# A two-layer transformer block on one core: order of the score maxima, weight splits and output projection, the first keys in two halves, and the rotation's halves exchanged by transfers

## The reference

```python
xn = _layernorm(x)
x = x + attn0(xn) + ffn0(xn)      # softmax(q k / 4) v, then Wo; gelu(xn W1 + b1) W2 + b2
xn = _layernorm(x)
x = x + attn1(xn) + ffn1(xn)      # below; silu(x1) * x2, then w3

def _rope(x, cos, sin):           # on q and k of layer 1
    x1, x2 = jnp.split(x, 2, axis=-1)
    rot = jnp.concatenate([-x2, x1], axis=-1)
    return x * cos + rot * sin
```

## Time and profile before

| | us |
|---|---|
| median of 3 runs | 607.77 |
| lowest, highest | 606.92, 608.82 |
| profiled execution, whole | 603.88 |
| its span | 602.2 |
| PE busy in the span | 566.0 |
| DVE busy | 456.7 |
| ACT busy | 348.2 |
| POOL busy | 234.2 |

### The profile page before, as it was taken

The page is one execution under the profiler, slowest core; times in us unless marked ns, Lnnn a source line. Parts: engine busy times, 40 slices in busy tenths (PEclk is TensorE's granted clock), DMA queues, the critical chain, the costliest instruction groups (busy, mean ns, idle before and its releaser), DMA issues.

```text
span 602.2 us, 10503 instructions
## 1 busy us (share of the span) xinstructions
PE 566.0 (94%) x3216; PEld 435.4 (72%) x3216; DVE 456.7 (76%) x1232; ACT 348.2 (58%) x598; POOL 234.2 (39%) x345
## 2 busy tenths in 40 slices
PE   4899899999999999999999998989989999998997
PEld 3797567877777878668777676867667778775764
DVE  6499876856466687476898687798989889789673
ACT  3666746673564673675674666447645664556451
POOL 6143414623203421213223114354745486455242
PEclk9989999999999999999999999999999999999999
DMA  6987442244223244315434314335443354444101
GB/s 199 128 247 226 119 116 81 80 140 109 89 67 107 82 129 124 89 41 170 124 123 123 89 47 130 89 90 129 136 108 87 99 161 130 106 124 113 29 3 70
DMA packets 30535, 67.02 MB, mean 111 GB/s; under 512 B 4880, under 2 KB 18192, under 8 KB 28560
## 3 DMA queue, kind: packets, MB, share of 16 engines
q1 hardware_dynamic: 21840, 38.04, 24.3%
q0 software_dynamic: 8640, 28.32, 15.7%
HBM read 50.87 MB, written 13.63 MB: 107 GB/s over the span
## 4 chain that ended last, share of the span: by engine, by line
PE 69%; DVE 12%; issue 6%; DMA 5%; ACT 5%; POOL 2%; SPq 0%; DVEq 0%; ACTq 0%; POOLq 0%
PE banks L763 47%; PE banks L823 7%; PE banks L849 6%; PE banks L871 6%; DMA q_sb<-max_t 3%; DVE banks L1153 2%; DMA q_sb<-stage 1%; DVE x_res L1197 1%; ACT L1004 1%; DVE hid L1218 1%; PE banks L783 1%; PE banks L852 1%; POOL probs L705 1%; DVE bn L1051 1%; ACT hid_f L1005 1%
## 5 line engine op out<-in xcount | busy, mean ns | idle before, releaser
L985 ACT ACTIVATE probs<-banks 128x512 f32<-128x512 f32 (+1 forms) x256 | 138.0, 545 | 184.9 <-PE banks L849 150.1
L763 PE MATMUL banks<-xnT,w_up 128*128 128x512 f32 x576 | 151.6, 397 | 0.1
L1158 DVE TENSOR_REDUCE neg_max<-banks 128x2 f32<-128x512 f32 x128 | 87.5, 688 | 78.0 <-PE banks L823 76.2
L763 PE MATMUL banks<-w_down,hid 128*128 128x512 f32 x480 | 127.9, 400 | 5.7 <-ACT hid_f L1005 2.0
L763 PEld LDWEIGHTS banks<-xnT,w_up 128*128 128x128 f32 x576 | 101.6, 189 | 27.5 <-issue 10.3
L763 PEld LDWEIGHTS banks<-w_down,hid 128*128 128x128 f32 x480 | 85.3, 189 | 33.4 <-DVE neg_max L1158 8.9
L1153 DVE CUSTOM_DVE_ANT_0 banks<-banks,mask_qk 128x128 f32<-128x128 f32 (+1 forms) x256 | 86.4, 375 | 29.9 <-PE banks L823 29.4
L823 PEld LDWEIGHTS banks<-k_sb,q_sb 96*128 96x128 f32 x512 | 93.1, 193 | 22.0 <-issue 3.4
L823 PE MATMUL banks<-k_sb,q_sb 96*128 96x256 f32 (+1 forms) x512 | 100.4, 278 | 4.2 <-DMA q_sb<-stage 2.0
L705 POOL TENSOR_SCALAR_AFFINE_SELECT probs<-probs 128x256 f32<-128x256 f32 x128 | 61.8, 483 | 78.2 <-ACT probs L985 71.7
L849 PE MATMUL banks<-q_sb,k_sb 97*128 97x512 f32 x192 | 79.2, 412 | 9.9 <-DMA q_sb<-max_t 6.4
(11 more groups left out here) (79 smaller groups left out, 657.1 us busy)
## 6 DMA issues: line engine op xcount, KB each, us to landing
q_sb<-q_parts SPq DMA_DIRECT2D x60, 256.0 KB, 4.4
raw<-in_up POOLq DMA_DIRECT2D x48, 256.0 KB, 3.1
raw<-in_down POOLq DMA_DIRECT2D x40, 256.0 KB, 3.0
q_parts<-stage SPq DMA_DIRECT2D x30, 256.0 KB, 2.5
raw<-in_attn POOLq DMA_DIRECT2D x20, 256.0 KB, 3.6
k_parts<-stage SPq DMA_DIRECT2D x14, 256.0 KB, 2.5
k_sb<-k_parts SPq DMA_DIRECT2D x14, 256.0 KB, 4.0
out<-x_res SPq DMA_DIRECT2D x8, 256.0 KB, 2.2
```

Source lines behind the costliest of these rows:

```text
L763: mm = nc.tensor.matmul(out_ap, lhs(a), rhs(b_), start=first and j == 0, stop=stop and j == 2, **kw)
L985: nc.scalar.activation(probs[:, i, 0:w], banks[:, ST_BANKS[k % 2], 0:w], ACT.Exp, scale=SCALES[n // B]).then_inc(exp_done, 1)
L1158: nc.vector.tensor_reduce(neg_max[:, s, 2 * g:2 * g + 2, t], banks[:, bank_of[x], :].rearrange("p (r t) -> p r t", r=2)[:, :, 0:w], AX.X, ...
```

## The change

Six edits. (1) `mt` and `mrow` are appended earlier and count to the head of slot 5, so they stand ahead of the due steps. (2) The `w_out` splits of layer 0, four in slot 7 of unit 0 before, go one each to slot 7 of units 0 to 3. (3) In layer 0 the eight parts of `up` stand ahead of `wo`. (4) The first keys go in two halves of four transfers of 64 source partitions: groups 0 to 3 ahead of the first queries, groups 4 to 7 between the two halves of these; layer 0's key weights and the two places that store and load its keys are permuted to suit. (5) `turn` comes four slots after `qkv` and not two, `round` and `store` five and not four. (6) ACT starts two transfers behind its drain that put each half of `qkv_v` into the other half of `rot_b`; the two sine products of DVE go, and `turn` first multiplies `rot_b` by the sines in one instruction of 128 partitions, then adds. The signs in the sine table move with it. ACT's drain then also waits for POOL's last rounding (`staged_lo`), which DVE did before.

```diff
     if x[0] == "qkv":
-        return [(1, ("drain", x)), (2, ("turn", x)), (4, ("round", x)), (4, ("store",) + x[1:])]
+        return [(1, ("drain", x)), (4, ("turn", x)), (5, ("round", x)), (5, ("store",) + x[1:])]
...
-        head = [k for k, x in enumerate(slot) if x[0] in ("st", "m")]
+        head = [k for k, x in enumerate(slot) if x[0] in ("st", "m", "mt", "mrow")]
...
+        if i == MT_SLOT and u + 1 < UNITS:
+            slots[i] += [("mt", u + 1), ("mrow", u + 1)]
...
-    if u + 1 < UNITS:
-        slots[5] += [("mt", u + 1), ("mrow", u + 1)]
...
-        fill = parts(("wo", n - 1, 0)) + parts(("wo", n - 1, 1)) + fill
+        k = 8 if u < LU else 0
+        fill = fill[:k] + parts(("wo", n - 1, 0)) + parts(("wo", n - 1, 1)) + fill[k:]
...
-    if u == 0:
-        slots[7] += split(0, "attn", 6, 7, 8, 9)
+    if u < S:
+        slots[7] += split(0, "attn", 6 + u)
...
             if k == 2:
-                eng.wait_ge(first_k, 64)
+                for f in range(2):
+                    eng.wait_ge(first_k[f], 64)
...
+            def first_keys(f):
+                k = stg[("store", 0, 2)]
+                for h in range(2):
+                    for e in range(2):
+                        at = 32 * h + 16 * e
+                        sp_.dma_start(k_sb[at:at + HD, 4 * f:4 * f + 4, :].bitcast(F32),
+                                      stage[64 * f:64 * f + 64, k % 2, h, 0, :].bitcast(F32)).then_inc(first_k[f], 16)
...
+                            if j == 0:
+                                first_keys(1)
...
                         if n:
                             pe.wait_ge(k_loaded[f], 16 * n)
                         else:
-                            pe.wait_ge(first_k, 64)
+                            pe.wait_ge(first_k[f], 64)
...
                     ins.then_inc(wk_copied, 1)
+                    if n >= B:
+
+                        act.wait_ge(wk_copied, cp[x] + 1)
+                        if hips[x]:
+                            act.wait_ge(staged_lo, hips[x])
+                        nc.scalar.dma_start(rot_b[0:64, 0:w, :], qkv_v[64:P, 0:w, :]).then_inc(swapped, 16)
+                        nc.scalar.dma_start(rot_b[64:P, 0:w, :], qkv_v[0:64, 0:w, :]).then_inc(swapped, 16)
...
-                    dve.wait_ge(rot_sin, 2 * hips[x] + 2)
+                    dve.wait_ge(c_loaded, 48)
+                    dve.wait_ge(swapped, 32 * (hips[x] + 1))
+                    nc.vector.tensor_tensor(rot_b[:, 0:w, :], rot_b[:, 0:w, :],
+                                            table[:, 1:2, :].to_broadcast([P, w, T]), ALU.mult).then_inc(rot_sin, 1)
+                    dve.wait_ge(rot_sin, hips[x] + 1)
```

More of the change, by code:

```diff
@@ L37 @@
 RAW = 4
+MT_SLOT = 5
 RING = 3
@@ L111, in with_followers @@
 def with_followers(slots):
-    due = [[] for _ in range(len(slots) + 5)]
+    due = [[] for _ in range(len(slots) + 7)]
     o = []
     for g, slot in enumerate(slots):
-        head = [k for k, x in enumerate(slot) if x[0] in ("st", "m")]
+        head = [k for k, x in enumerate(slot) if x[0] in ("st", "m", "mt", "mrow")]
         cut = head[-1] + 1 if head else 0
@@ L447, in build @@
         m_loaded = [sem(f"m_loaded{k}") for k in range(RING)]
-        first_k = sem("first_k")
+        first_k = [sem(f"first_k{f}") for f in range(2)]
         first_q = [sem(f"first_q{j}") for j in range(2)]
+        swapped = sem("swapped")
         st_filled = sem("st_filled")
@@ L584, in _ @@
                     if x == ("store", 0, 2):
-                        for h in range(2):
-                            for e in range(2):
-                                at = 32 * h + 16 * e
-                                sp_.dma_start(k_sb[at:at + HD, :, :].bitcast(F32),
-                                              stage[:, k % 2, h, 0, :].bitcast(F32)).then_inc(first_k, 16)
+                        first_keys(0)
                     elif x == ("store", 0, 0):
@@ L602, in _ @@
                         for j in range(2):
-                            dst = kscr[n].rearrange("(h e) d (g t) -> e (d g) h t", e=2, g=NKV)[j]
+                            if n < B:
+                                dst = kscr[n].rearrange("q d x -> q (d x)").rearrange("(h e) (p t) -> e p h t", e=2, t=T)[j]
+                            else:
+                                dst = kscr[n].rearrange("(h e) d (g t) -> e (d g) h t", e=2, g=NKV)[j]
                             sp_.dma_start(dst, stage[:, k % 2, :, 0, :].bitcast(F32)).then_inc(staged[k % 2], 16)
@@ L621, in _ @@
                     g = slice(4 * f * T, (4 * f + 4) * T)
+                    if n < B:
+                        src = kscr[n].rearrange("q d x -> q (d x)").rearrange("q (f d x) -> f q d x", f=2, d=HD)[f]
+                    else:
+                        src = kscr[n].rearrange("q d x -> (q d) x")[:, g]
                     sp_.dma_start(k_sb[0:4 * HD, 4 * f:4 * f + 4, :].rearrange("p g t -> p (g t)").bitcast(F32),
-                                  kscr[n].rearrange("q d x -> (q d) x")[:, g]).then_inc(k_loaded[f], 16)
+                                  src).then_inc(k_loaded[f], 16)
                 if x[0] == "mrow":
@@ L1108, in _ @@
                                             stage[:, k % 2, 0, 0:w, :].bitcast(F32), ALU.subtract).then_inc(wk_emptied, 1)
-                if x[0] == "drain" and x[1][0] == "qkv" and x[1][1] >= B:
-                    x = x[1]
-                    _, n, pair = x
-                    w = 2 if pair < 2 else 1
-                    dve.wait_ge(wk_copied, cp[x] + 1)
-                    dve.wait_ge(c_loaded, 48)
-                    if hips[x]:
-                        dve.wait_ge(staged_lo, hips[x])
-                    other = table[:, 1:2, :]
-                    nc.vector.tensor_tensor(rot_b[0:64, 0:w, :], qkv_v[64:P, 0:w, :],
-                                            other[64:P].to_broadcast([64, w, T]), ALU.mult).then_inc(rot_sin, 1)
-                    nc.vector.tensor_tensor(rot_b[64:P, 0:w, :], qkv_v[0:64, 0:w, :],
-                                            other[0:64].to_broadcast([64, w, T]), ALU.mult).then_inc(rot_sin, 1)
                 if x[0] == "turn":
@@ L1239, in _layouts @@
     block = (REP + 2) * HD
-    w0 = np.concatenate([i["L0_attn_Wq"][q_rows(lambda h: h * HD)], i["L0_attn_Wk"][kd(lambda g: g * HD)],
+    k0 = np.array([(4 * f + g) * HD + d for f in range(2) for d in range(HD) for g in range(4)])
+    w0 = np.concatenate([i["L0_attn_Wq"][q_rows(lambda h: h * HD)], i["L0_attn_Wk"][k0],
                          i["L0_attn_Wv"][gd(lambda g: g * HD)]])
@@ L1258, in _layouts @@
     row = np.arange(P) // 8
-    rope = np.stack([cos[row % 8], np.where((row < 8)[:, None], sin[row % 8], -sin[row % 8])], 1).astype(np.float32)
+    rope = np.stack([cos[row % 8], np.where((row < 8)[:, None], -sin[row % 8], sin[row % 8])], 1).astype(np.float32)
     c = np.ascontiguousarray
```

## The result

The changed kernel takes **625.68 us** (median of 4 runs, 624.6 to 628.1) where the kernel before takes 608.3 beside it: a ratio of **1.031**, 95% interval 1.027 to 1.036, so 3% slower. The ratio is taken over fast runs alone, so it differs a little from the quotient of the two medians, 1.029. The forecast of 602.2 and its range of 595.0 to 608.8 are both missed, on the wrong side. The profiled execution took 628.07, its span 626.3 us against 602.2.

The account below looks back on a forecast made before the run. PE was taken as the bound, busy 566.0 of 602.2 us, so only its 36.2 us of idle time could be won. Terms +3.3 - 3.3 - 1.6 - 0.5 - 3.5 = -5.6 moved the median 607.77 to 602.2; range 595.0 to 608.8.

Parts of the forecast that it names:

- First keys in halves, +3.3: Start: queries land 2.9 us earlier, but ScalarE's third drain waits for keys and delays the first `m`; loss of 3.3 us.
- Splits of `w_out`, `up` ahead of `wo`, -3.3 and -1.6: Unit 1's waits of PE go, -3.3 us; layer 0's waits for a GELU, 2.0 us together, mostly go, -1.6.
- -0.5 for the maxima: Maxima ahead of due steps, outside the rotation's stretch: part of PE's 6.4 us of waits goes, -0.5 us.
- The rotation, -3.5: Units at 380 to 546: -4.7 us together with the maxima, against 0.7 for ScalarE's issues and 0.5 for `mrow`; net -3.5.
- 9.7 had been expected: Of the 12.9 us of work leaving VectorE over twelve rotations, 9.7 fall in the stretch from 380 to 546.
- half of the 9.35: PE idles 9.35 us in 380 to 546; half goes by the rotation and the maxima together, -4.7 us.
- VectorE was all of it: Rival, units at 380 to 546: all 9.35 us of PE's idle time go, instead of 3.5 net; 596.3 us, chance 0.11.
- The 0.5 for `mrow` behind the store: Rotation units: `mrow` stands behind the rotation's later store on SyncE; cost taken as 0.5 us.
- the store holds the maxima: Rival, rotation units: late store delays `mrow`, six times 1.08, 6.5 us, if rounding ends after maxima's copy; 608.7, chance 0.17.
- The exchange is late: Rival, rotation units: VectorE's turn waits for the transfers, 1.1 us nine times, 10 us; 612.2 us, chance 0.13.
- The rule on the shared port: VectorE's new product costs 618 ns by the rows, 951 if taking turns with GpSimd, giving back about 1.0 us: 603.2.

Follow-up runs that it names:

- e1: Changed kernel with each of layer 0's six half-key loads made four transfers of 16 partitions: 613.56 us, ratio 1.0097 to the kernel before.
- e3: Changed kernel with the first keys in halves undone, including order, store and load of layer 0's keys: 610.25 us, ratio 1.0049 to the kernel before.
- e12: Kernel before with only the first three edits (maxima, `w_out` splits, `up` ahead of `wo`), a repeat of e7: 596.87 us, ratio 0.9833.
- e2: Changed kernel with the rotation's store six slots after its projection instead of five: 620.41 us, ratio 1.0208 to the kernel before.
- e4: e3 with the rotation's store one slot later: 603.96 us, ratio 0.9950 to the kernel before.
- e9: e5 without the exchange transfers, the product reading `qkv_v` itself: 620.72 us, ratio 1.0228 to the kernel before.
- e5: Kernel before with only the rotation's two edits (later slots; exchange by transfers and one product): 622.76 us, ratio 1.0255.
- e6: Kernel before with only the rotation's later slots, its two products left in place and no exchange: 613.16 us, ratio 1.0097.
- e10: e3 with the rotation's rounding and store both one slot later: 610.34 us, ratio 1.0058 to the kernel before.
- e7: Kernel before with only the first three edits (maxima, `w_out` splits, `up` ahead of `wo`): 597.32 us, ratio 0.9838.

## Why the prediction was wrong, step by step

- **First keys in halves, +3.3.** The start was right in mechanism, and each of its times came within 1.0 us. Its size is less sure. The 2.9 of e1 against e3 is near the term, but the traces put only 0.9 of it at the start; the +4.1 of the first section compares two single executions, and the same start varies by nearly as much (last section). The step that failed is the other half of that edit. The prediction says nothing of the new order in which layer 0's keys are stored and loaded, and so costs it at nothing; the diff shows it, six loads with a source of four rows. It cost 13.0, nearly as much as the rotation.
- **Splits of `w_out`, `up` ahead of `wo`, -3.3 and -1.6.** Right in sign and too small. Unit 1 gained 5.1, that is all three waits and what lay in smaller ones; units 5, 9 and 13 gained 3.3 together, more than the 2.0 of the waits for the GELU. With -0.5 for the maxima the sum was -5.4, and -9.8 and -10.1 were measured.
- **The rotation, -3.5.** Wrong in sign: +13.1 beside the other three edits (e3 against e12), +15.5 alone. Its premise held in part: VectorE lost 14.0 us of work, 6.5 of them in layer 1, where 9.7 had been expected. But the step "half of the 9.35" failed. It took a wait's place for granted: a busy share of 88% was read as the cause of the waits, and the work that went stood in a unit's first slots, while the product that came stands in the slot ahead of the row maxima. In unit 16 the copy of the maxima comes 0.5 us later by that place, and TensorE's wait grows as much. How that place makes all of the 8.0 is not shown: in unit 23 the landing grew and not the copy's delay, and most of the time is the clock behind the waits. With VectorE's work gone and TensorE's idle time in layer 1 up from 15.7 to 24.6, the rival "VectorE was all of it" is out as well. The 0.5 for `mrow` behind the store measured 6.0 to 6.3 (e2, e4).
- **The rival "the store holds the maxima"** had mechanism and point of decision right: in unit 23 the store starts at 508.13, behind the copy of the maxima at 507.83. Its sum of 6.5 is close to the 6.0 and 6.3 measured, but by luck: it counted six waits of 1.08, and the store lengthened three of 2.6 to 2.7. Behind one of these, in unit 17, the clock fell to 0.50 in the changed kernel, which the prediction left out. "The exchange is late" did not come true with four slots (2.8 us of waits) and did with two (29.3). ScalarE's two issues took 0.47 and 0.92 us at the median, not 0.425 each; by e9 against e5 that made no difference that can be told.
- **The rule on the shared port** (the Trainium skill, SBUF — State Buffer, section "SBUF: two separate sides"): the new product averages 742 ns, between the 618 of the rows and the 951 of the rule. Single ones take 1.27 in the changed kernel and 1.78 in e9, the latter beside a GpSimd addition of two operands that began 0.05 us earlier; the product ends 0.55 after it. The trace agrees with the rule.

The sum as measured: +13.0 loads, +2.9 the rest of the first keys' edit, +13.1 rotation, -10.1 the other three: +18.9, the ratio of 1.031. The parts are differences along one row of kernels, so they must add up to it. By the intervals they stand to some 3 us each, and they come from different chips.

## What to carry to other kernels

When a layout is "permuted to suit", read every transfer that touches it as a new instruction with a new form, and look at who stands behind it in its queue. Taking work off an engine helps only where that engine is waited for: compare the place of the work that goes with the place of the work that comes, against the one result the bottleneck needs next. A wait of two or three microseconds on the main engine can cost twice its length when the clock falls behind it, so price it by rows that show what came after; the same length of wait can also cost nothing more.

## What the runs showed of the hardware

- One transfer of 256 KB from four long rows delays the loads behind it by microseconds: a query load took up to 11.5 us from issue to landing in the changed kernel, 6.5 in e1 and 7.5 before.
- In layer 1 one wait of 1.70 (e6) was followed by a clock of 1.00 and one of 2.70 (e9) by 0.50, 1.2 GHz, over the five microseconds behind it. The length of the wait alone does not decide it: the 2.62 of the changed kernel in unit 23 and a 2.99 in e10 were followed by 1.00, and in e3 a 2.67 by 1.00 and a 2.57 by 0.66.
- The same code starts in two ways: the first `st` waits 0.50 for the first row of maxima in e7 and 4.39 in e12, and unit 0 then takes 16.24 or 17.70, in e12 at a clock of 0.50 from 42 to 44. The landing of that one small transfer decides it. Issued at 34.72 in e12, it lands after 6.8 us, with the DMA share at 1.01 from 36 to 42; issued at 36.46 in e7, after 2.9; issued at 37.93 before, with a share of 0.08 from 38 to 40, after 1.8. In the seven traces that issue it by 35.4 it takes 4.5 to 6.8 and lands at 39.3 to 41.7, so an earlier first `m` gained little. Why the other traffic stands there stays open.
